# Two-layer Perceiver block: L0 attention in double steps, context parts kept between layers

## The reference

```python
x = x + _L0_xattn_ref(_layernorm(x), ctx_768, ...)
x = x + _L0_attn_ref(_layernorm(x), ...)
x = x + _L0_ffn_ref(_layernorm(x), ...)
x = x + _L1_xattn_ref(_layernorm(x), ctx_768, ctx_768, ...)
...
def _L0_xattn_ref(x, context, ...):          # 16 heads of 64
    q_in = x @ Wq + _lora(x, ...)
    k_in = org_ctx @ Wk + _lora(org_ctx, ...)
    v_in = org_ctx @ Wv + _lora(org_ctx, ...)
    out = _attention(q_in, k_in, v_in)       # softmax(q k^T / 8) v
...
def _L1_xattn_ref(query, key, value, ...):   # 16 heads of 16
    K = _l2norm(key @ Wk + bk)
    V = value @ Wv + bv
```

## Time and profile before

| what | us |
|---|---|
| median of 3 runs (2086.05 to 2088.25) | 2086.76 |
| the profiled execution, its own time | 2086.96 |
| its span in the profile | 2085.3 |
| start to L0 attention | 94 |
| L0 attention, first pieces and loop | 94 to 1175 |
| token mixer and mixture of L0 | to 1406 |
| L1 keys and values, twice | 66 each |
| L1 attention, twice | 132 each |
| the rest of L1 | from 1802 |

### The profile page before, as it was taken

The page is one execution under the profiler, slowest core; times in us unless marked ns, Lnnn a source line. Parts: engine busy times, 40 slices in busy tenths (PEclk is TensorE's granted clock), DMA queues, the critical chain, the costliest instruction groups (busy, mean ns, idle before and its releaser), DMA issues. The chain is left out here.

```text
span 2085.3 us, 33327 instructions
## 1 busy us (share of the span) xinstructions
PE 1888.4 (91%) x13464; PEld 1269.3 (61%) x13464; DVE 1096.4 (53%) x1550; ACT 1031.0 (49%) x1363; POOL 650.1 (31%) x315
## 2 busy tenths in 40 slices
PE   6899999999899999999999776868998999766999
PEld 2576766667566676666766544448544844443887
DVE  3577586675665767667562244247100800374565
ACT  1244444444554444444442232116897799625443
POOL 1026565555544656556564212002000100010000
PEclk9899999999999999999999888788999999977999
DMA  5510000000300000000020100004463355400220
GB/s 185 142 46 6 6 16 1 16 6 6 97 1 16 6 6 16 1 16 6 1 74 7 61 0 1 18 15 112 74 105 66 81 92 97 107 1 1 92 97 35
DMA packets 89922, 90.59 MB, mean 43 GB/s; under 512 B 29928, under 2 KB 79824, under 8 KB 86448
## 3 DMA queue, kind: packets, MB, share of 16 engines
q1 hardware_dynamic: 88736, 87.46, 17.3%
q10 hardware_dynamic: 1040, 1.05, 0.2%
HBM read 58.57 MB, written 8.91 MB: 32 GB/s over the span
## 5 line engine op out<-in xcount | busy, mean ns | idle before, releaser
L760 POOL TENSOR_TENSOR sums<-sums,probs 128x1024 f32<-128x1024 f32 x224 | 534.7, 2387 | 354.8 <-ACT probs L793 305.1
L844 DVE TENSOR_REDUCE part_max<-psum_banks 128x2 f32<-128x1024 f32 (+1 forms) x256 | 312.8, 1224 | 125.8 <-PE psum_banks L1006 121.3
L793 ACT ACTIVATE probs<-psum_banks 128x1024 f32<-128x1024 f32 x240 | 245.9, 1024 | 123.2 <-PE psum_banks L1052 116.0
L1066 PE MATMUL psum_banks<-probs,values 128*64 128x256 f32 x2048 | 278.4, 393 | 0.3 <-ACT probs L796 0.3
L771 ACT ACTIVATE keys<-psum_banks 64x512 fp32r<-64x512 f32 x256 | 151.6, 592 | 239.0 <-PE psum_banks L979 235.9
L2472 ACT ACTIVATE probs<-psum_banks,k_inv_norm 128x1024 f32<-128x1024 f32 x256 | 257.9, 1260 | 1.3 <-PE psum_banks L2487 1.2
L837 DVE TENSOR_TENSOR keys<-psum_banks,keys 64x512 fp32r<-64x512 f32 x256 | 176.4, 689 | 116.8 <-ACT keys L771 110.8
L1066 PEld LDWEIGHTS psum_banks<-probs,values 128*64 128x64 f32 x2048 | 124.5, 136 | 99.8 <-issue 60.1
L1034 PEld LDWEIGHTS psum_banks<-q_hi,keys 128*128 128x128 f32 x1024 | 138.0, 189 | 76.7 <-issue 51.7
L1034 PE MATMUL psum_banks<-q_hi,keys 128*128 128x256 f32 x1024 | 184.6, 302 | 0.0
L776 ACT ACTIVATE values<-psum_banks 128x512 f32<-128x512 f32 x128 | 76.5, 598 | 192.7 <-PE psum_banks L991 192.7
(11 more groups left out here) (443 smaller groups left out, 3036.3 us busy)
## 6 DMA issues: line engine op xcount, KB each, us to landing
k_pairs<-keys SPq DMA_DIRECT2D x192, 128.0 KB, 4.2
ctx_tok<-in_ctx SPq DMA_DIRECT2D x16, 384.0 KB, 3.5
wk_pair<-wkv_parts SPq DMA_DIRECT2D x16, 256.0 KB, 3.0
wv_quad<-wkv_parts SPq DMA_DIRECT2D x8, 512.0 KB, 3.8
w_gate_up<-in_L_ffn_gate_proj_w SPq DMA_DIRECT2D x8, 512.0 KB, 4.0
w_gate_up<-in_L_ffn_up_proj_w SPq DMA_DIRECT2D x8, 512.0 KB, 5.0
...
```

The source lines that it names most:

```text
L760: pool.tensor_tensor(sums[:, :, :, :], probs[:, 0, :, :, :] if step == 1 else sums[:, :, :, :], probs[:, step % SLOTS, :, :, :], ALU.add). ...
L793: act.activation(probs[:, step % SLOTS, :, :, :], scores, ACT.Exp, scale=SCALE0).then_inc(p_ready, 1)
L844: dve.tensor_reduce(part_max[:, :, i, c], psum[:, bank:bank + 2, 0:width], AX, ALU.max).then_inc(m_read, 1)
L1066: last = pe.matmul(psum[rows(h), 3, 0:L], values[:, kt, at:at + HD0], probs[:, step % SLOTS, h, j, :], start=kt == 0, stop=kt == KT - 1, t ...
```

## The change

A double step g now does steps 2g and 2g + 1 together: on TensorE the key piece first, both `begin_scores`, both shifts and low products, the first maximum piece, both weighings, the denominators at a unit's end, `spread_maxima`, the second maximum piece, and then values or turns. Of the pieces behind, the first goes to bank 0 and the second to bank 1. The spread goes to bank 0. The high queries are made on ScalarE. The reciprocal of a unit's denominators is taken in quarters of 64 columns, in even units one in each of four double steps. GpSimd halves `sums` by one more add, so two matmuls make the denominators.

In L0, SP stores `cA_hi`, `cA_lo` and `cB` of each batch (2 MB each) to a DRAM tensor. In L1 the chunks of these parts are loaded into four slots, three loads a chunk, from chunk 4 on each after the values of the chunk four before it; the tokens, the transposes (L541), the two copies and the two subtractions are gone, and the loops are written out. `project_keys` waits for the loads only. The twelve loads of the keys' first half stand in SP's list between chunk 5 and chunk 6, and wait there for the split keys of chunk 3.

```diff
+        self.context_parts = nc.dram_tensor("ctx_parts", (B, 3, P, N), F32, kind="Internal").ap()
...
+def keys_at(m, c):
+
+    return (m - 1) * TWOS + c - 2
+
+
+def spread_at(m):
+
+    return m * TWOS - 2
+
+
+def high_queries_at(m, h):
+
+    return (m - 2) * TWOS + 1 + h
+
+
+def low_queries_at(m, h):
+
+    return (m - 1) * TWOS + (3 + h if m % 2 == 0 else -1)
+
+
+def pieces_of_double_steps():
+
+    ahead, top, behind = ({g: [] for g in range(FIRST, END)} for _ in range(3))
     for m in range(1, UNITS):
         for c in range(CHUNKS):
+            g = max(keys_at(m, c), FIRST)
             if (m, c) != (1, 0):
-                second[key_step(m, c)].append(("keys", m, c))
+                ahead[g].append(("keys", m, c))
             for i in range(2):
-                top[max_step(m, c, i)].append(("max", m, c, i))
+                top[g].append(("max", m, c, i))
     for c in range(CHUNKS):
-        first[turn_step(c)].append(("turn_a", 0, c))
-        behind[turn_step(c)].append(("turn_b", 0, c))
+        behind[(PAIRS - 2) * TWOS + c] += [("turn_a", 0, c), ("turn_b", 0, c)]
     for quad in range(1, UNITS // 2):
-        for step in range(0, STEPS, 2):
-            first[(2 * quad - 1) * STEPS + step + 1].append(("values", quad, step))
-            behind[(2 * quad - 1) * STEPS + step + 1].append(("values", quad, step + 1))
-    return first, second, top, behind
+        for c in range(TWOS):
+            behind[(2 * quad - 1) * TWOS + c] += [("values", quad, 2 * c), ("values", quad, 2 * c + 1)]
+    return ahead, top, behind
...
+    SUMS = STEPS
+    QUARTERS = 4
...
+    in_bank0 = [("keys", 0, CHUNKS - 2), ("spread", 0), ("keys", 1, 0)]
+    in_bank1 = [("max", 0, CHUNKS - 1, 0)]
+    for g in range(FIRST, END):
+        in_bank0 += ahead[g] + [("spread", m) for m in range(1, UNITS) if g == spread_at(m)] + behind[g][:1]
+        in_bank1 += top[g] + behind[g][1:]
+    previous = {**dict(zip(in_bank0[1:], in_bank0)), **dict(zip(in_bank1[1:], in_bank1))}
...
+                def keep_parts(b):
+                    for i, part in enumerate((cA_hi, cA_lo, cB)):
+                        sp.dma_start(core.context_parts[b, i, :, :], part[:, :].bitcast(F32)).then_inc(parts_kept[b], 16)
...
+                keep_parts(0)
...
+                    if m == PAIRS + 2:
+                        sp.wait_ge(ctx_lo, 2 * CHUNKS)
+                        keep_parts(1)
...
+                        sp.wait_ge(parts_kept[0], 48)
...
+                    pool.wait_ge(summed, n * SUMS + STEPS - 1)
+                    pool.tensor_tensor(sums[:, :, 0, :], sums[:, :, 0, :], sums[:, :, 1, :], ALU.add).then_inc(summed, 1)
...
-                for g in range(FIRST_STEP, LAST_STEP):
-                    for piece in first[g] + second[g]:
+                for g in range(FIRST, END):
+                    for piece in ahead[g]:
                         prepare(piece)
-                    if g < LAST_STEP - 1:
-                        weights((g + 1) // STEPS, (g + 1) % STEPS)
+                    if g < END - 1:
+                        for step in (2 * g + 2, 2 * g + 3):
+                            weights(step // STEPS, step % STEPS)
                     for piece in behind[g]:
                         prepare(piece)
-                    if g == LAST_STEP - STEPS + 8:
+                    for m in range(2, UNITS):
+                        for h in range(2):
+                            if g == high_queries_at(m, h):
+                                high_queries(m, h)
...
-                        dve.tensor_copy(q_hi[rows(half), m % Q_SLOTS, h, :], q[rows(h), :]).then_inc(q_hi_ready, 1)
...
+                    if m >= 2:
+                        dve.wait_ge(s_done, (m - 1) * STEPS)
...
+                def invert(n, quarter):
+                    columns = slice(quarter * L // QUARTERS, (quarter + 1) * L // QUARTERS)
+                    dve.wait_ge(raw_kept, n + 1)
+                    dve.reciprocal(raw[:, 1, columns], raw[:, 1, columns]).then_inc(inv_ready, 1)
+
+                def scale_raw(n):
+                    dve.wait_ge(inv_ready, (n + 1) * QUARTERS)
+                    dve.tensor_tensor(queries_of(n), raw[:, 0, :], raw[:, 1, :], ALU.mult).then_inc(out_kept, 1)
+
                 def divide(n):
-                    dve.wait_ge(raw_kept, n + 1)
-                    dve.reciprocal(raw[:, 1, :], raw[:, 1, :]).then_inc(inv_ready, 1)
-                    dve.wait_ge(inv_ready, n + 1)
-                    dve.tensor_tensor(queries_of(n), raw[:, 0, :], raw[:, 1, :], ALU.mult).then_inc(out_kept, 1)
+                    for quarter in range(QUARTERS):
+                        invert(n, quarter)
+                    scale_raw(n)
...
+                    for piece in ahead[g] + top[g][:1]:
+                        prepare(piece)
+                    if g >= END - TWOS:
+                        keep_output_part(2 * (g % TWOS))
+                    for m in range(1, UNITS):
+                        if g == spread_at(m):
+                            shifts(m)
+                    if g // TWOS % 2 == 0 and g >= 2 * TWOS:
+                        if 1 <= g % TWOS <= QUARTERS:
+                            invert(g // TWOS - 1, g % TWOS - 1)
+                        if g % TWOS == QUARTERS + 1:
+                            scale_raw(g // TWOS - 1)
+                    for piece in top[g][1:]:
                         prepare(piece)
                     for m in range(1, UNITS):
+                        if g == keys_at(m, CHUNKS - 1):
                             maxima(m)
                     for piece in behind[g]:
                         prepare(piece)
                     for m in range(1, UNITS):
                         for h in range(2):
+                            if g == low_queries_at(m, h):
                                 low_queries(m, h)
+                    if g % (2 * TWOS) == TWOS:
+                        divide(g // TWOS - 1)
+                    if g >= END - TWOS:
+                        keep_output_part(2 * (g % TWOS) + 1)
...
-                    for j in range(2):
-                        for h in range(2):
-                            last = pe.matmul(psum[rows(h), 3, L:2 * L], core.ones[:, 0:HD0], sums[:, h, j, :],
-                                             start=j == 0, stop=j == 1, tile_position=(0, HD0 * h))
+                    for h in range(2):
+                        last = pe.matmul(psum[rows(h), 3, L:2 * L], core.ones[:, 0:HD0], sums[:, h, 0, :],
+                                         start=True, stop=True, tile_position=(0, HD0 * h))
...
+                    next_two = (2 * g + 2, 2 * g + 3) if g < END - 1 else ()
+                    for piece in ahead[g]:
                         prepare(piece)
-                    if g >= LAST_STEP - STEPS:
-                        output_part(g % STEPS)
-                    for piece in second[g]:
-                        prepare(piece)
-                    for m in range(1, UNITS):
-                        if g == spread_step(m):
-                            spread_maxima(m)
-                    if ahead is not None:
-                        shift_scores(ahead // STEPS, ahead % STEPS)
-                        finish_scores(ahead // STEPS, ahead % STEPS)
+                    if g >= END - TWOS:
+                        output_part(2 * (g % TWOS))
+                    for step in next_two:
+                        begin_scores(step // STEPS, step % STEPS)
+                    for step in next_two:
+                        shift_scores(step // STEPS, step % STEPS)
+                        finish_scores(step // STEPS, step % STEPS)
                     for piece in top[g][:1]:
                         prepare(piece)
                     if g >= 0:
-                        weigh(g // STEPS, g % STEPS)
+                        for step in (2 * g, 2 * g + 1):
+                            weigh(step // STEPS, step % STEPS)
+                        if g % TWOS == TWOS - 1:
+                            denominators(g // TWOS)
+                    for m in range(1, UNITS):
+                        if g == spread_at(m):
+                            spread_maxima(m)
                     for piece in top[g][1:]:
                         prepare(piece)
                     for piece in behind[g]:
                         prepare(piece)
-                    if g >= 0 and g % STEPS == STEPS - 1:
-                        denominators(g // STEPS)
+                    if g >= END - TWOS:
+                        output_part(2 * (g % TWOS) + 1)
...
-                sp.sem_inc(turned, 2)
-                with sp.Fori(0, CHUNKS // 2) as i:
-                    for slot in range(2):
-                        c = i * 2 + slot
-                        sp.wait_ge(turned, c + 1)
-                        load_tokens(sp, core, tok[:, slot, :, :], b, bass.ds(c * CHUNK, CHUNK), arrived[slot])
-                if b == 0:
-                    sp.wait_ge(pairs_padded, 2)
```

(20 more changed lines are left out.)

213 lines of the change are left out of this document (71 added, 142 removed).

## The result

The changed kernel takes 2033.76 us (median of 4 runs, 2032.0 to 2035.26) where the kernel before, run beside it, takes 2087.51: a ratio of 0.974, with an interval of 0.9725 to 0.9759. That is 54 us less; 66 were forecast. 2033.8 lies inside the range of 2002 to 2056 and also inside the forecast case A. The profiled execution has a span of 2031.3 us against 2085.3.

What follows compares the result with a forecast made beforehand. TensorE was taken to bound L0's attention loop (busy 1017 of 1038 us), with 0.17 us lost per change of tile form. L0's -58 and L1's -8 sum to -66 us, from 2086.76 to 2021; range 2002 to 2056.

Steps and rivals of the forecast that it cites:

- case A: Whole kernel: the forecast itself, 2003 to 2037 us; chance 0.66 counted with two other cases in its range.
- Streaming plus changes of form: L0 double steps: 5.29 us of streaming plus four changes of tile form at 0.17 us make 5.97 us.
- the wait for bank 1: L0 odd units: second value piece waits 0.15 us for VectorE to read the maximum, making double steps 8.43 us.
- No wait on the maxima, no wait for GpSimd but at the end: L0 units: TensorE's waits on maxima under 0.2 us in even units; denominators wait for GpSimd only in unit 15.
- B: L0 double steps: first maximum read 0.6 us later than reckoned, price 38 us, 2037 to 2070 us; chance 0.20.
- C: L0 double steps: maximum one whole reduction late, TensorE waits 0.9 us each, 113 us, 2134 us total; chance 0.06.
- The covers: L0: slack of 0.3 us before TensorE wants the first maximum's bank, and 0.9 us for GpSimd's sums before the denominators.
- Unit 14: L0 unit 14, whose last two double steps have neither keys nor maxima: 4 us gained.
- The start: L0 loop start: four round trips of 1.71 us for unit 1's first maxima, some 8 us idle; unit 0 ends 3 later.
- Unit 6: L0 unit 6, turning the second batch's context: 2.1 us more a double step over 49.1, so 66 us, gain 2.
- Unit 15: L0 unit 15: four output-part waits of about 1.0 us, GpSimd 3 us more, fewer form changes save 4; 3 us slower.
- L1: L1 keys and values: chunks of 5.65 us, start 2 us better, 2.8 us wait before chunk 6; 8 us gained in all.

Runs made afterwards that it cites:

- the order with two more changes: Changed kernel with first products, shift and low products of one step, then the same of the other: 2077.89 us, ratio 0.9946.
- the new L1 alone: Kernel before with the context-part stores and the new L1 keys and values, old L0 attention: 2081.7 us, ratio 0.9962.
- the new L0 alone: Changed kernel with the old L1 keys and values and no context-part stores: 2042.9 us, ratio 0.9773.
- the reordered kernel: Changed kernel with SP's twelve key-pair loads in L1 put behind the loads of chunk 7: 2022.09 us, ratio 0.9675.

## Why the prediction was right, and where it was off

**Streaming plus changes of form: right.** 5.97 us a double step was forecast and 5.99 is measured. The unit lengths by copies mislead a little: in VectorE's list the copy that ends an even unit stands behind a maximum (694.38, 2.21 after its denominators), the one that ends an odd unit behind the low queries of the unit after next as well (644.51, 3.85 after them). From first products to first products (645.47, 694.39, 763.77) an even unit is 48.9 us, forecast 49.1, and an odd one 69.4, forecast 68.7; the pair is 118.3 for 117.8. The odd units' 0.7 is the second value piece: 8.56 us a double step, 8.43 forecast. It starts 0.34 us after the row before it (700.17 to 700.51), and its next row 0.34 later (700.85), where 0.24 and 0.23 are usual: the wait for bank 1, forecast as 0.15, costs 0.2.

What the gain of an odd unit is made of, the forecast took from the total of 74.85 and didn't name. The kernel before has waits in these units, seven in each, of the key piece for ScalarE's copy of the value piece that shares its bank:

```profile
329.75 0.73 PE L979 MATMUL psum_banks<-cA_hi,wk_pair 128*128 128x512 f32 x2 [0.21 <-ACT values L776]
```

From the first products to this row it is 0.86 us (328.89 to 329.75) where four matmuls of 256 columns stream in 0.46: 0.4 each time, 2.8 a unit. By first products an odd unit gains 5.5, an even one 3.3. Each has sixteen changes of form fewer, an estimated 3.0 us if each costs the 0.19 that the order with two more changes shows for its kind; the odd unit has the 2.8 of waits besides, and its new wait for bank 1 takes back 1.6. What is left is the shorter denominators.

**No wait on the maxima, no wait for GpSimd but at the end: right.** B and C needed a late maximum, and no maximum piece waits for one in the units. The covers that the prediction named, 0.3 us and 0.9, were enough. How thin the first was, the kernel with high queries on VectorE shows. At the end of unit 14 the denominators do wait, 0.75 us; in unit 15 3.32, where 1.53 + 3 was forecast.

**Unit 14: right**, 4.0 for 4.

**The start: the step that failed most.** "TensorE idles some 8 us; a little of that is idle today: unit 0 ends 3 us later." The 7.3 us of idle time were right, and the window of before has 1.0 of it. The netting to 3 was wrong: nothing else paid for it, since this stretch has only 0.8 us less work. And the 3.4 us of the low clock were not in the sum at all. Together 5.9 us too little.

**Unit 6: off by 2.3, and the step itself was right.** 2.06 us more for a double step with turns (8.05 against 5.99) was forecast as 2.1. (49.1 and eight times 2.1 are the 66 of the forecast; against 68.75 that is 2.75 less, entered as 2.) By first products the unit takes 68.0 (508.07 to 576.09). One double step takes 10.4, between its first maximum scores and the next ones (550.63 to 561.00):

```profile
552.31 1.80 DVE L894 TENSOR_TENSOR qT<-raw_out 128x256 f32<-128x256 f32 x1
...
555.29 0.66 PE L1043 MATMUL psum_banks<-ident,cB 128*128 128x128 f32 x4 [1.39 <-DVE part_max L861]
...
558.24 1.79 PE L1064 MATMUL psum_banks<-q_hi,keys 128*128 128x256 f32 x8
...
679.17 1.82 DVE L894 TENSOR_TENSOR qT<-raw_out 128x256 f32<-128x256 f32 x1
```

The multiplication that ends the division takes 1.80 us in VectorE's list ahead of the maximum. It isn't special to unit 6: in unit 8, the last row, it is 1.82, and as long in the other even units. There TensorE wants the bank only 3.8 us later and nothing waits. In the odd units, where it stands at the end of a double step, the same row is 0.43. GpSimd is adding from 551.47 to 556.3 and from 678.33 to 683.3, and has nothing to do at 702.30, when the one in unit 9 runs. By the Trainium skill ("SBUF — State Buffer", SBUF: two separate sides), VectorE with two SBUF inputs and GpSimd exclude each other from a shared pair of ports for a whole instruction; the two durations agree. The maximum is read 1.39 us late for the second turn, where 0.74 is the rule in this unit, and then the first products take 1.79 for 1.11: the clock again, 0.65 and 1.7 us of the 2.3. The kernel with the sums not halved separates the two; its row of the same wait, and the first products behind it:

```profile
559.86 0.66 PE L1041 MATMUL psum_banks<-ident,cB 128*128 128x128 f32 x4 [1.40 <-DVE part_max L859]
...
561.95 1.11 PE L1062 MATMUL psum_banks<-q_hi,keys 128*128 128x256 f32 x8
```

The wait is there, the low clock isn't, and unit 6 takes 68.0 from copy to copy for 69.1, though the other even units are 0.45 longer there. In the kernel with the high queries on VectorE it is the same, with 67.5.

**Unit 15: right in size by two errors that cancel.** 7 us of waits less 4 of saved changes was the forecast, 3. Idle time grew by 5.8: four waits on the output parts of 4.1 in all, forecast as about 4, and 1.8 more for GpSimd, forecast as 3. The stretches at the low clock are 6.8 us long before and 15.2 after, which costs 4.2 more, and the work at full clock is 6.5 shorter (73.66 - 3.4 against 71.35 - 7.6). The saving was underrated and the clock not counted.

**L1: the mechanism and its place right, its size short.** The chunk was forecast at 5.65 and is 5.56. The start gained 4.6 us where 2 were forecast (chunk 1 starts 246.3 us after L0's last copy, before 250.9; 246.7 with the new L1 alone, 251.4 with the new L0 alone). The wait before chunk 6 was forecast as 2.8 us a batch, 0 to 6, and is 3.35 and 3.89. But the low clock around it takes another 1.7 and 4.3 us (7.22 and 9.85 for 5.56). Without wait and clock L1 gives 20 us; the two take 13 of it back, and the reordered kernel, 14 us faster, has neither.

**In sum**, the 12 us that the profile misses of the forecast are 5.9 in the start, 1.7 in the units 1 to 5 and 7 to 13, 2.3 in unit 6, 0.5 in unit 15 and 1.6 in L1 (less than L1's time scatters from kernel to kernel). Behind the last two stand larger amounts that cancel: more low clock around new waits costs 3.4 us in the start, 1.7 in unit 6, 4.2 in unit 15 and 6.0 in L1, 15 in all, and none of it was in the sum; shorter work in unit 15 and L1's better start and chunks paid most of it. The term that was missing is the clock.
